# Loading inputs 2 and 3 of the next quad in front of the stores of graphs 2 and 3 instead of behind them

## What is computed

```python
q = (x @ Wq + bq).reshape(b, n, H, HD)      # k and v likewise
scores = einsum('bqhd,bkhd->bhqk', q, k) / sqrt(HD) + (1 - adj) * -1e9
attn = softmax(scores, axis=-1)
out = einsum('bhqk,bkhd->bqhd', attn, v).reshape(b, n, d)
x = layernorm(x + out @ Wo + bo)            # layer 0
x = layernorm(x + out)                      # layer 1, its own q, k, v
```

## Time and profile before

| what | value |
|---|---|
| time, median of 3 runs | 2998.36 us (2998.1 to 2999.74) |
| the profiled execution's own time | 2996.24 us |
| its span, first to last instruction | 2994.4 us |
| mean granted clock of PE | 0.993 |
| PE busy | 2939.3 us (98%) |
| DVE busy | 1815.3 us (61%) |
| ACT busy | 1495.2 us (50%) |
| POOL busy | 1358.2 us (45%) |
| transfers | 417.70 MB, mean 139 GB/s |

### The profile page before, as it was taken

How to read it: one execution, slowest core, us unless ns; L and a number is a source line. 1 busy time by engine, 2 the same in 40 slices (tenths; PEclk the granted TensorE clock), 3 DMA queues, 4 the chain that set the end, 5 groups by cost and what they waited for, 6 DMA issues and landing times.

```text
span 2994.4 us, 58006 instructions
## 1 busy us (share of the span) xinstructions
PE 2939.3 (98%) x18956; PEld 2478.4 (83%) x18956; DVE 1815.3 (61%) x7060; ACT 1495.2 (50%) x5007; POOL 1358.2 (45%) x1285
## 2 busy tenths in 40 slices
PE   7999999999999999999999999999999999999996
PEld 5888888888888888888888788888888888888885
DVE  3565656566555656465656666666766666676665
ACT  4444445454545444444545455555555555555552
POOL 2445545455555554554545534334434333443442
PEclk9999999999999999999999999999999999999997
DMA  5344453534344444444354445556555555655555
GB/s 188 89 123 131 114 141 106 148 106 134 110 132 113 135 117 124 131 115 140 107 148 141 131 132 161 160 167 169 147 144 155 161 159 167 170 150 142 155 161 156
DMA packets 411007, 417.70 MB, mean 139 GB/s; under 512 B 46112, under 2 KB 308512, under 8 KB 410656
## 3 DMA queue, kind: packets, MB, share of 16 engines
q1 hardware_dynamic: 409408, 413.32, 49.3%
q10 hardware_dynamic: 1296, 0.67, 0.1%
HBM read 145.37 MB, written 103.81 MB: 83 GB/s over the span
## 4 chain that ended last, share of the span: by engine, by line
PE 95%; issue 1%; ACT 1%; DVE 1%; SPq 1%; DMA 1%; POOL 0%; POOLq 0%; DVEq 0%; ACTq 0%
PE ring L330 46%; PE ring L338 34%; PE ring L362 8%; PE ring L373 7%; ACT prob L489 1%; SPq L233 0%; DMA prob<-w_k 0%; DMA x_raw<-x_feat 0%; DVE prob L578 0%; SPq L227 0%; SPq L244 0%; POOL norm L746 0%; POOL xt_lo L729 0%; DVE w_lo_k L547 0%; DVE w_lo_o L541 0%
## 5 line engine op out<-in xcount | busy, mean ns | idle before, releaser
L489 ACT ACTIVATE prob<-prob,neg_max 128x128 f32<-128x128 f32 x2048 | 792.1, 393 | 114.4 <-DVE neg_max L578 114.4
L739 POOL TENSOR_TENSOR prob<-prob,inv_sum 128x512 f32<-128x512 f32 x512 | 538.1, 1077 | 591.7 <-DVE inv_sum L586 591.5
L469 ACT ACTIVATE k_all<-ring,bk_col 128x512 f32<-128x512 f32 x256 | 311.7, 1217 | 690.0 <-PE ring L330 690.0
L578 DVE CUSTOM_DVE_ANT_0 prob<-ring,mask 128x128 f32<-128x128 f32 x2048 | 440.7, 284 | 312.2 <-PE ring L362 312.0
L729 POOL TENSOR_TENSOR xt_lo<-x_raw,xt_hi 128x512 fp32r<-128x512 f32 x196 | 261.6, 1346 | 444.9 <-DVE xt_hi L553 444.9
L476 ACT ACTIVATE q_all<-ring,bq_col 128x512 f32<-128x512 f32 x256 | 176.5, 689 | 486.4 <-PE ring L330 486.4
L338 PE MATMUL ring<-w_hi_v,xt_hi 128*128 128x512 f32 x1024 | 406.9, 397 | 8.3 <-DVE neg_max L578 8.3
L330 PE MATMUL ring<-xt_hi,w_hi_k 128*128 128x512 f32 x1024 | 399.4, 390 | 13.5 <-DVE w_lo_k L541 13.5
L338 PE MATMUL ring<-w_hi_v,xt_lo 128*128 128x512 f32 x1024 | 399.4, 390 | 0.0
L330 PE MATMUL ring<-xt_lo,w_hi_k 128*128 128x512 f32 x1024 | 399.3, 390 | 0.0
L338 PE MATMUL ring<-w_lo_v,xt_hi 128*128 128x512 f32 x1024 | 399.1, 390 | 0.0
(11 more groups left out here) (67 smaller groups left out, 4720.1 us busy)
## 6 DMA issues: line engine op xcount, KB each, us to landing
prob_t<-turned SPq DMA_DIRECT2D x1024, 128.0 KB, 2.7
x_res<-x_tok SPq DMA_DIRECT2D x256, 256.0 KB, 3.7
x_raw<-x_feat SPq DMA_DIRECT2D x196, 256.0 KB, 3.3
x_feat<-x_turned SPq DMA_DIRECT2D x512, 64.0 KB, 2.1
x_tok<-x_bias SPq DMA_DIRECT2D x128, 256.0 KB, 2.3
at_lo<-x_bias SPq DMA_DIRECT2D x256, 64.0 KB, 2.1
at_lo<-x_turned SPq DMA_DIRECT2D x256, 64.0 KB, 2.1
out<-x_bias SPq DMA_DIRECT2D x64, 256.0 KB, 4.2
```

The lines of the kernel that those rows point to most:

```text
L469: act.activation(k_all[:, m, :].rearrange("p (b j n) -> p b n j", b=QB, n=SQ), ring[K_BANK[m]][:].rearrange("p (b n j) -> p b n j", b=QB, ...
L489: last = act.activation(prob[b][:, i, n, :], prob[b][:, i, n, :], ACT.Exp, bias=neg_max[b][:, i, n:n + 1], scale=-1.0, accum_out=row_sum[b ...
L578: last = dve.tensor_tensor_reduce(prob[b][:, i, n, :], score_bank(b, i)[:, n, :], mask[layer][:], -SCALE, BIG, ALU.add, ALU.min, neg_max[b ...
L739: pool.tensor_tensor(prob[b][:, i], prob[b][:, i], inv_sum[b][:, i, :].unsqueeze(2).to_broadcast([P, NC, NODES]), ALU.mult).then_inc(norm_ ...
```

## The change

In SP's step, the two `load_raw` of inputs `early` to 3 of quad `s + 1` are moved from behind `finished(f, 2)` and `finished(f, 3)` to in front of them. In step 31 they are also moved in front of the loads of the new key weights. In steps 0 and 1 there is no quad `f`, and from step 34 on the moved loop is empty, so the order differs in steps 2 to 33. The waits inside `load_raw`, `finished` and `turn_probs` stay as they are, as does the order on every other engine.

```diff
                 if la is not None:
                     turn_probs(a, 3)
+                if nxt is not None:
+                    for b in range(early, QB):
+                        load_raw(s + 1, b, nxt)
                 if lf is not None:
                     finished(f, 2)
                     finished(f, 3)
                 if s == G - 1:
                     sp.wait_ge(w_next_out, 16 * 3)
                     sp.wait_ge(k_done, NC * G)
                     for h in range(2):
                         load_next("k1", h)
-                if nxt is not None:
-                    for b in range(early, QB):
-                        load_raw(s + 1, b, nxt)
                 if s == G - 1:
                     sp.wait_ge(q_done, NC * G)
```

## The result

The changed kernel takes 2991.57 us (median, 2989.95 to 2993.03, 12 runs), the kernel before 2998.76 us (2996.24 to 3000.14, 12 runs): a ratio of 0.9978 with a 95% interval of 0.997 to 0.9986. The profiled execution took 2991.24 us, span 2989.4 us.

The account below looks back on a forecast made before the run. PE bounds the kernel, busy 98%; only step 32 can gain, 4.02 us of gap plus 1.75 us of clock, 5.77 in all. From 2998.36 this gives 2992.6 us, own range 2991.4 to 2993.9, all cases 2990.4 to 2996.2.

Parts of the forecast that it names:

- the clock's part: Step 32, attends behind PE's gap: 1.75 us lost because the clock ran at 1.2 instead of 2.4 GHz.
- no busier than usual: Step 32, 1671 to 1677 us: transfers 0.66 busy, so the moved loads were taken to land in 3.4 us.
- Ordinary steps at 0 us: 31 of the 32 steps: inputs finish earlier, but DVE's mask waits for PE's scores anyway, so 0 us.
- Step 31 at 0 us: Step 31: new key weights load some 3 us later, but ACT needs them only about 20 us later, so 0 us.
- DVE had the low parts of the new weights to make: Step 32: this work until 1651.7 us brings DVE to cast 0 only 7.5 us before the scores.
- A: Step 32: loads land later, leaving a gap up to 0.9 us, perhaps 1.75 of clock; 2992.7 to 2995.2 us; chance 0.11.
- B: Moved loads: they do not really come sooner or lose their time elsewhere, no effect, 2998.4 us; chance 0.07.
- C: Every layer-0 step: graph 3's `x_res` is held up, finally delaying PE's output projection; above 3020 us; chance 0.04.
- C's first link: Layer-0 steps: SP's wait holds up `x_res` of graph 3, for which POOL's `add_out_bias` waits; 9 us to spare at PE.
- D: Step 32: timed runs, 2.12 us longer than the profiled one, hold a longer gap; 2990.5 us; chance 0.04.

Follow-up runs that it names:

- the best version: The changed kernel, with quad 1's input casts put before the low parts of the output weight on DVE in step 0: 2982.98 us.
- short low parts: The kernel before, old order, with DVE making the new weights' low parts for only 8 of 1024 columns: 2995.75 us, ratio 0.9991.

## Why the prediction was right

**The place and the mechanism: right, and shown.** It was said that only step 32 holds time that the change can give back, that the gap closes to nothing and that the clock's part comes back with it. The period went from 56.94 to 51.17 us, the new order in step 32 alone gives 2991.74 us, and the old order without the change of weights 2991.95, all beside the changed kernel's 2991.57. The issues were forecast for 1671.5 and 1672.8 (measured: both between 1671.57 and 1673.14), the end of the casts for up to 1677.6 (1676.4). The scores of this execution begin 0.66 us later than in the one before, so against them the loads go out 4.94 us ahead (forecast 4.35), and the first is cast after 2.7 us (3.4). The casts are over in time for the mask to wait for the scores, and its first half is done 1.30 + 0.97 = 2.27 us after they begin, where PE needs it at 3.84: 1.6 us to spare, forecast 1.1. For the landing the forecast called transfers that are 0.66 busy "no busier than usual"; the earlier trace rows show no other stretch to compare with, so that step was an assumption. It did no harm: in the changed kernel they are 0.55 busy there.

**The size.** Forecast 2992.6 us, measured 2991.57, in the range given; 5.77 us of gain against 7.2 between the medians, whose interval reaches from about 4.2 to 9.0 us. Step 32 in three executions of the kernel before has 5.77, 4.44 and 6.26 us of excess, 5.5 on average, so the term was sized well. That the single execution it was read from lies this near the average is luck: another one would have given 4.44. The spans of these three average 2995.8 us, those of the two kernels with a closed gap and full weights (2989.4, 2988.3) 2988.85: a difference of 6.95. Of the 1.5 us beyond step 32, 1.0 lies ahead of step 1 (first key copy at 69.2 against 68.15 us on average) and 0.4 behind the last key copy. The order of SP is the same in both stretches, and kernels of either order are found at both ends, so I take it for scatter; more executions would be needed to show it. Nor is it settled whether the gain exceeds 0.2% (6.0 us), to which the prediction gave 0.34: the medians say 7.2 us, their interval reaches below 6.0, and the direct comparison of the new order in step 32 alone gave 6.3.

**Ordinary steps at 0 us: right.** DVE's wait for inputs fell by 192 us (forecast about 155) and reappears as waits for PE.

**Step 31 at 0 us: wrong.** The step looked only at the new key weights, which do have time. It overlooked that the inputs of that step also stood behind them, that the mask was late by 1.1 us, and that ACT, DVE and SP hand such a lateness on to step 32. Against the first execution of the kernel before the gap is 1.2 to 1.6 us shorter without it, against the other two (2.94 and 3.54 us) 0.1 to 1.1. The sum is not harmed, because the new order in step 32 closes the gap with or without it: the two contributions overlap and do not add.

**Why DVE was late: half right.** "DVE had the low parts of the new weights to make" named the place. With that work almost removed the gap was still 3.0 us; DVE's queue waits out ACT's high parts. Only with both short, and the load of the new value weights left out, did the lateness go; which of these last two counts more was not tried. The prediction also gave DVE's late arrival at cast 0 (7.5 us before the scores instead of 15.6) as what sets step 32 apart, without saying how it reaches the mask. DVE then stood idle for 11.74 us; its lateness acts through SP, whose queue waits for the probabilities that DVE turns, so that the loads go out 1.55 us after the scores instead of 6.65 us before them as in step 20.

**Rivals.** A (a gap remains), B and C did not occur. C's first link is in the trace: POOL waits 54.4 us in all for `x_res`. It is at most 3.4 us at a time, and PE has no wait at L338 in any ordinary step. D, a longer gap in the timed runs, is not borne out by the two further executions, 2.94 and 3.54 us.

## What to carry to other kernels

Look for the step whose period is longer than its neighbours', not for the engine with the most waiting: of 395 us of waits for loads this change took away 192, and the kernel gained some 6 us by it, all in one step. Where two weight sets change over, conversions in an in-order queue hold everything behind them, also the queue of an engine that waits for their engine, so a load that is harmlessly late elsewhere becomes the bound there; put transfers that someone waits for in front of stores that nobody does. Contributions to one gap do not add, so undo each alone and keep each alone before sharing out a gain. And one gap can differ by 1 us between executions of the same kernel (here 2.94 to 4.02 us), so a difference of that size needs more than one pair of traces.

## What the runs showed of the hardware

The clock behind a gap is not a function of the gap's length alone. Two kernels with nearly the same gap, PE's timeline at the first attends. New order in step 31 alone, gap 2.43 us, the 16 attends take 1.98 us and the period has 1.60 us more than the gap explains:

```profile
1682.14 1.98 PE L376 MATMUL ring<-prob_t,v_first 128*64 128x128 f32 x16 [2.43 <-DVE neg_max L581]
```

New order everywhere but in step 32, gap 2.84 us, the same 16 in 1.09 us at the full clock:

```profile
1684.01 1.09 PE L376 MATMUL ring<-prob_t,v_first 128*64 128x128 f32 x16 [2.84 <-DVE neg_max L581]
```

The longer gap kept 2.4 GHz, the shorter one fell to 1.2. The Trainium skill (TensorE: Matmul & The Clock Gate, "What's actually happening") says that the point at which the clock changes depends on when in the chip's own cycle the work falls; these rows agree. Nor does the fall have to come in the gap: with short low parts (gap 3.00 us) the first 16 attends still take 1.09 us, and the 48 behind them 4.46 us, where the changed kernel needs 2.79. What a fall costs here was 1.50 to 2.72 us in five executions, and gaps of 0.57 and 1.32 us, and the 1.85 us in step 0 of the best version, kept the full clock. Beyond this, moving a wait on SP cost nothing measurable in 31 steps, although it put two more SP waits in front of 12 issues in each: in step 20 SP has 15 us free behind these issues, and there a wait of 1 to 2 us leaves no trace at PE.
